# One decoder layer with cross attention and experts on one core: GpSimd's routing and norm application go to ScalarE, DMA and VectorE, and every fourth head's probabilities are turned by TensorE

## The chip, the cores and the metric

The kernel runs on one core of a Trainium2 chip. The metric is the device time of one execution in microseconds. Three runs of the kernel before took 1084.84, 1085.49 and 1087.52 us; the median is 1085.49.

## The reference

The input `x` is 32 x 64 x 256 and the context `ctx_2048` has the same shape, so there are 2048 tokens of width 256. Three sublayers follow each other, each on the layer norm of its input and each added to it.

```python
x = x + attn(_layernorm(x))              # 16 heads attend to one another inside each token, with rope
x = x + xattn(_layernorm(x), ctx_2048)   # 2048 queries against 2048 keys, 16 heads of 16
x = x + moe(_layernorm(x))               # a shared expert, and the best 2 of 8 routed ones
```

In the cross attention queries, keys, probabilities and values are quantised: q and k per row to 127 steps, the probabilities unsigned to 255 steps of the row's largest, v to 127 steps. In the expert layer each token has a sigmoid score per expert; the two experts whose score plus bias is largest are chosen, and the token times its score goes through the expert's `silu(x w1) * (x w3)` and `w2` in bf16.

## The kernel before, in words

128 tokens are a tile, so there are 16 tiles. A prologue prepares keys and values of the whole context in SBUF. Then `over_tiles` runs a body 18 times. The body is written once for each engine, by hand, and each engine executes its list strictly in order and waits on semaphores. In body `t` four tiles are worked on at once: the cross attention of tile `t`; the preparation of `a = t + 2` (first norm, q, k, v, rope, the scores inside a token) and of `n = t + 1` (values inside a token, output projection, second norm, queries); the end of the attention, the third norm and the routing of `m = t - 1`; the experts of `o = t - 2`. The 16 heads `h` of tile `t` are the clock of the body: everything else hangs on a head number.

For one head TensorE makes 128 x 2048 scores in two halves (`scores`, L1528). Each half is a slot of 1024 words in PSUM, and there are two slots, used in turn (`score_uses`, `wait_slot`). VectorE evicts each half with its minimum (`keep_scores`, L1178) and makes a bias (`bias`, L1188). ScalarE takes the exponential (`exp_head`, L865) into `prob`, a ring of four. SP issues a DMA that turns the 128 x 2048 fp16 rectangle into `prob_t`, a ring of six (`turn`, L431). TensorE multiplies four heads at a time by the values (`times_values`, L1558).

GpSimd's list for a tile, in order: `ln_scale(0, a)`, `value_products(2, n)`, `spread_sums(m)`, which waits for VectorE's `cross_sum` (`sum_inv`, L1195) at head 3, `value_products(3, n)` and folds, `rope(a)`, `norm_ho(n)`, `score_products(0, a)`, `ln_scale(2, m)`, more products and folds, `ln_scale(1, n)`, `choose(m)`, folds, `route(0, m)`, `shift_scores(a)`, `route(1, m)`, `value_products(0, a)` and `(1, a)`, folds. `shift_scores(a)` waits for VectorE's `largest_score(a)` (`hs_max`, L1119), which stands just ahead of head 15's eviction. `ln_scale(kind, t)` makes the inverse deviation from VectorE's statistics (`var_eps` L462, `rstd` L466) and applies the norm (`normed`, L482). TensorE turns `normed` (`ln_turn`, L1391) and ScalarE copies it out (`ln_keep`, L809).

`choose` ranks the eight scores of a token in 12 instructions on GpSimd (L523 to L556). TensorE spreads the gates over the partitions at heads 13 and 14 (`spread_gates`, L1605), ScalarE copies them to SBUF (`keep_gates`, L916), and GpSimd multiplies the turned tokens by them (`route`, L567) into `routed_t`. `experts(i, j)` multiply four experts each (L1386): (0, 0) at head 14 of body `m + 1`, the others at heads 0 and 1 of the next body. ScalarE takes their tanh (`hidden_tanh`, L923): group 0 at head 14, group 1 at the start of head 0. VectorE forms the product (`expert_hidden`, L1235 and L1238): group 0 at head 0, group 1 at head 1. Then follow `experts_out` and `add_out` at head 2. The last tile has its own forms on VectorE (`choose_last`, `route_last`).

Of the kernel before, what the change touches and what calls it, by code (L numbers as in the profile page):

```python
# [36 lines left out]
F32 = mybir.dt.float32  # L37
# [26 lines left out]
POOL_NORMS = (0, 1, 2)  # L64
BY_DMA = tuple(range(H))
# [70 lines left out]
def layer_kernel(nc, a):  # L136
    with ExitStack() as ctx:
# [14 lines left out]
        earlier = sb("earlier", [P, E, E])  # L152
# [87 lines left out]
        gate = sb("gate", [P, 3, E])  # L240
        ahead = sb("ahead", [P, E, E])
        beats = sb("beats", [P, E, E])
        ties = sb("ties", [P, E, E])
        routed_gate = sb("routed_gate", [P, E])
        last_gate = sb("last_gate", [P, 4, E])

        routed_both = sb("routed_both", [P, 2, E * D], BF16)
        gate_wide = routed_both[:, 0, :].bitcast(F32).rearrange("p (e q) -> p e q", e=E)
# [110 lines left out]
        last_chain = sem("last_chain")  # L359
        gate_spread = sem("gate_spread")  # L360
        gate_kept = sem("gate_kept")
        routed_kept = sem("routed_kept")
# [19 lines left out]
        def _(sp):  # L382
# [15 lines left out]
            for buf, name in ((w_o, "w_o"), (w_xq, "w_xq"), (b_xq, "b_xq"), (w_p, "w_p"),  # L398
                              (b_p, "b_p"), (w_gate, "w_gate"), (b_expert, "b_expert"),
                              (earlier, "earlier"), (w_s1, "w_s1"), (w_s3, "w_s3"),  # L400
                              (w_s2, "w_s2")):
                sp.dma_start(buf[:], a[name]).then_inc(w_loaded, 16)
# [29 lines left out]

            def body(t):
                for h in range(H):
                    if t.exists() and by_dma(h):
                        turn(h, t)
                    if h == 9 and (t + 3).exists():
                        load_x(t + 3)
                    if h == 4 and (t + -2).exists():
                        store(t + -2)  # L440
# [8 lines left out]
        def _(pool):  # L449
# [5 lines left out]
            def ln_scale(kind, t):  # L455
# [3 lines left out]
                if kind not in POOL_NORMS and (due := t.due(1)) is not None:  # L459
                    pool.wait_ge(ln_done[kind], due)  # L460
                    pool.sem_inc(settled, 1)
# [8 lines left out]
                if kind not in POOL_NORMS:  # L470
                    pool.tensor_scalar(shift[:, kind:kind + 1], mean_var[:, kind, 0:1],
                                       rstd[:, kind:kind + 1], -1.0, ALU.mult, ALU.mult
                        ).then_inc(ln_shifted[kind], 1)
                    return
                if kind > 0:
                    pool.wait_ge((one_done, two_done)[kind - 1], t.count(1, 1))
                    pool.sem_inc(settled, 1)
                if (due := t.due(1)) is not None:
                    pool.wait_ge(ln_turned[kind], due)
                    pool.sem_inc(settled, 1)  # L480
# [30 lines left out]

            def choose(t):


                pool.wait_ge(gate_tanhed, t.count(1, 1))
                pool.sem_inc(settled, 1)
                if (due := t.due(2)) is not None:
                    pool.wait_ge(gate_spread, due)
                    pool.sem_inc(settled, 1)
                sig, biased, rank = gate[:, 0, :], gate[:, 1, :], gate[:, 2, :]  # L520
                mine = biased.unsqueeze(2).to_broadcast([P, E, E])
                others = biased.unsqueeze(1).to_broadcast([P, E, E])
                pool.tensor_scalar(sig, gate_tanh[:], 0.5, 0.5, ALU.mult, ALU.add).then_inc(gate_chain, 1)  # L523
                pool.wait_ge(gate_chain, t.count(12, 1))
                pool.sem_inc(settled, 1)
                pool.tensor_tensor(biased, sig, b_expert[:], ALU.add).then_inc(gate_chain, 1)
                pool.wait_ge(gate_chain, t.count(12, 2))
                pool.sem_inc(settled, 1)
                pool.tensor_tensor(ahead[:], others, mine, ALU.subtract).then_inc(gate_chain, 1)
                pool.wait_ge(gate_chain, t.count(12, 3))  # L530
                pool.sem_inc(settled, 1)
                pool.tensor_scalar(ties[:], ahead[:], 0.0, None, ALU.is_equal).then_inc(gate_chain, 1)
                pool.tensor_scalar(beats[:], ahead[:], 0.0, None, ALU.is_gt).then_inc(gate_chain, 1)
                pool.wait_ge(gate_chain, t.count(12, 5))
                pool.sem_inc(settled, 1)
                pool.tensor_tensor(ties[:], ties[:], earlier[:], ALU.mult).then_inc(gate_chain, 1)
                pool.wait_ge(gate_chain, t.count(12, 6))
                pool.sem_inc(settled, 1)
                pool.tensor_tensor(beats[:], beats[:], ties[:], ALU.add).then_inc(gate_chain, 1)
                pool.wait_ge(gate_chain, t.count(12, 7))  # L540
                pool.sem_inc(settled, 1)
                pool.tensor_tensor(ties[:, :, 0:4], beats[:, :, 0:4], beats[:, :, 4:8], ALU.add
                    ).then_inc(gate_chain, 1)
                pool.wait_ge(gate_chain, t.count(12, 8))
                pool.sem_inc(settled, 1)
                pool.tensor_tensor(ties[:, :, 4:6], ties[:, :, 0:2], ties[:, :, 2:4], ALU.add
                    ).then_inc(gate_chain, 1)
                pool.wait_ge(gate_chain, t.count(12, 9))
                pool.sem_inc(settled, 1)
                pool.tensor_tensor(rank, ties[:, :, 4], ties[:, :, 5], ALU.add).then_inc(gate_chain, 1)  # L550
                pool.wait_ge(gate_chain, t.count(12, 10))
                pool.sem_inc(settled, 1)
                pool.tensor_scalar(rank, rank, 2.0, None, ALU.is_lt).then_inc(gate_chain, 1)
                pool.wait_ge(gate_chain, t.count(12, 11))
                pool.sem_inc(settled, 1)
                pool.tensor_tensor(routed_gate[:], rank, sig, ALU.mult).then_inc(gate_chain, 1)  # L556

            def route(i, t):

                pool.wait_ge(gate_kept, t.count(2, i + 1))  # L560
                pool.sem_inc(settled, 1)
                pool.wait_ge(ln_kept[2], t.count(1, 1))
                pool.sem_inc(settled, 1)
                if (due := t.due(4)) is not None:
                    pool.wait_ge(hidden_made, due)
                    pool.sem_inc(settled, 1)
                pool.tensor_tensor(routed_t[:, EG * i:EG * i + EG],  # L567
# [1238 lines left out]
```

## Time and profile before

| | |
|---|---|
| median of three runs | 1085.49 us |
| profiled execution | 1091.66 us |
| its span | 1089.9 us |
| mean granted TensorE clock | 0.865 |
| VectorE, GpSimd busy | 906.8, 854.3 us |
| TensorE matmul, ScalarE busy | 754.3, 686.6 us |
| DMA queue of SP, share of 16 engines | 72.4% |

The profiled execution is one run; its span is shorter than its time by what lies around it, 1.8 us. Busy shares are means over the whole run. PE is TensorE, DVE VectorE, ACT ScalarE, POOL GpSimd, SP the engine that issues the DMAs. A row of a timeline is start, duration, engine, line, operation, output and inputs, count, and in brackets how long the engine had been idle and what ended it.

### The profile page before, as it was taken

The page shows a single profiled execution, that of the slowest core. Times are in us where ns is not written, and L with a number is a line of the kernel's source. Part 1 is how long each engine was busy: PE and PEld are TensorE (multiplying, and loading weights), DVE is VectorE, ACT ScalarE, POOL GpSimd, SP SyncE. Part 2 cuts the span into 40 slices and gives each one's busy share as a digit, 9 for nine tenths or more (in the row PEclk, how much of TensorE's full clock was granted, in tenths as well). Part 3 has the DMA queues.
Part 4 walks back from the last instruction along what each step waited for, and adds up shares of the span by engine and source line. Part 5 has one row for each costly group of instructions (what it writes and reads, how often), then busy time and mean ns, then how long its engine had stood idle before and what let it go on. Part 6 is the DMA issues. An engine that isn't in the chain of part 4 may idle for free.

```text
span 1089.9 us, 21862 instructions
## 1 busy us (share of the span) xinstructions
PE 754.3 (69%) x7250; PEld 438.0 (40%) x7328; DVE 906.8 (83%) x1802; ACT 686.6 (63%) x843; POOL 854.3 (78%) x874
## 2 busy tenths in 40 slices
PE   7956667676667577676656777676768677677565
PEld 4533314344334344344333444344334344334244
DVE  4996889797979889796979889696978889798983
ACT  2534667675757667575768667575666667567761
POOL 7658989797988979797989979797988979763030
PEclk9975779897979989797989879797988979788988
DMA  6012879686986969596877869596876969588991
GB/s 221 1 39 66 163 130 171 125 166 116 167 146 121 168 117 167 111 168 118 163 143 138 159 117 172 106 168 117 162 146 118 178 115 168 97 160 150 165 175 24
DMA packets 540888, 147.71 MB, mean 136 GB/s; under 512 B 534116, under 2 KB 538727, under 8 KB 540391
## 3 DMA queue, kind: packets, MB, share of 16 engines
q1 hardware_dynamic: 540774, 146.31, 72.4%
q8 instruction: 58, 0.95, 0.4%
q14 instruction: 56, 0.45, 0.1%
HBM read 9.96 MB, written 2.10 MB: 11 GB/s over the span
## 4 chain that ended last, share of the span: by engine, by line
issue 31%; POOL 29%; PE 19%; DVE 16%; ACT 2%; POOLq 1%; DMA 1%; SPq 0%; DVEq 0%; ACTq 0%
POOL product L594 14%; DVE score L1178 8%; PE ps L1605 4%; PE ps L1386 4%; POOL normed L482 3%; PE ps_score L1528 3%; POOL folded L612 3%; POOL rstd L466 2%; POOL qk_sin L581 2%; PE ps_score L1386 2%; POOL qk_rot L583 2%; PE ps L1502 1%; PE ps L1507 1%; DVE q_parts L1161 1%; PE ps L1391 1%
## 5 line engine op out<-in xcount | busy, mean ns | idle before, releaser
L1178 DVE TENSOR_SCALAR_CACHE_REDUCE score<-ps_score,q_neg 128x1024 f32<-128x1024 f32 x512 | 636.4, 1276 | 92.6 <-PE ps_score L1528 92.6
L865 ACT ACTIVATE prob<-score,exp_bias 128x2048 uint16<-128x2048 f32 x256 | 512.1, 2001 | 100.8 <-DVE exp_bias L1188 94.5
L1528 PE MATMUL ps_score<-keys,queries 128*128 128x512 bf16 x946 | 319.9, 424 | 178.7 <-DVE score L1178 165.2
L1528 PEld LDWEIGHTS ps_score<-keys,queries 128*128 128x128 bf16 x1024 | 77.7, 103 | 308.9 <-DVE score L1178 239.3
L604 POOL TENSOR_TENSOR folded<-product 128x512 f32<-128x512 f32 x128 | 158.7, 1263 | 2.7 <-DVE hs L1114 1.7
L594 POOL TENSOR_TENSOR product<-hs_exp,v_tok 128x1024 f32<-128x1024 f32 x64 | 149.7, 2353 | 1.6 <-ACT hs_exp L830 1.6
L594 POOL TENSOR_TENSOR product<-qk_rot 128x1024 f32<-128x1024 f32 x64 | 149.0, 2342 | 0.2 <-POOL qk_rot L587 0.2
L567 POOL TENSOR_TENSOR routed_both<-normed_t,routed_both 128x1024 bf16<-128x1024 f32 x30 | 70.6, 2356 | 33.7 <-ACT routed_both L916 33.2
L612 POOL TENSOR_TENSOR folded<-folded 128x256 f32<-128x256 f32 x128 | 92.6, 746 | 0.0
L1391 PE MATMUL ps<-ident,normed 128*128 128x128 f32 x96 | 24.8, 347 | 89.1 <-POOL normed L482 82.5
L809 ACT COPY normed_t<-ps 128x256 f32<-128x256 f32 x48 | 17.6, 366 | 100.8 <-PE ps L1391 100.8
L1558 PEld LDWEIGHTS ps_pv<-prob_t,values 128*32 128x32 f16 x4096 | 60.1, 99 | 31.6 <-issue 31.6
L1558 PE MATMUL ps_pv<-prob_t,values 128*32 128x128 f16 x4096 | 71.4, 224 | 1.9 <-DMA prob_t<-prob 1.9
L1188 DVE TENSOR_SCALAR exp_bias<-low 128x1 f32<-128x1 f32 x256 | 53.9, 210 | 5.3 <-issue 0.3
L1391 PEld LDWEIGHTS ps<-ident,normed 128*128 128x128 f32 x96 | 12.0, 164 | 109.6 <-POOL normed L482 100.8
L916 ACT COPY routed_both<-ps 128x512 f32<-128x512 f32 x30 | 17.4, 584 | 60.0 <-PE ps L1605 59.7
L1386 PE MATMUL ps<-routed_both,w 128*128 128x128 bf16 x512 | 41.4, 227 | 18.2 <-POOL routed_both L567 13.9
L1605 PE MATMUL ps<-ident,routed_gate 128*128 128x128 f32 x256 | 54.0, 398 | 0.0
L1605 PEld LDWEIGHTS ps<-ident,routed_gate 128*128 128x128 f32 x256 | 52.1, 310 | 0.1
L1386 PEld LDWEIGHTS ps<-routed_both,w 128*128 128x128 bf16 x512 | 33.2, 102 | 41.5 <-POOL routed_both L567 28.8
L865 ACT ACTIVATION_READ_ACCUMULATOR prob<-score,exp_bias 128x1 f32 x256 | 48.2, 188 | 0.0
L462 POOL TENSOR_SCALAR var_eps<-mean_var 128x1 f32<-128x1 f32 x48 | 12.8, 267 | 38.8 <-DVE mean_var L1106 37.8
(138 smaller groups left out, 1216.2 us busy)
## 6 DMA issues: line engine op xcount, KB each, us to landing
prob_t<-prob SPq DMA_TRANSPOSE x256, 4.5
prob_t<-in_w SPq DMA_DIRECT2D x3, 1024.0 KB, 4.8
x_in<-in_x SPq DMA_DIRECT2D x16, 128.0 KB, 3.0
score<-in_cond_t SPq DMA_DIRECT2D x4, 512.0 KB, 6.9
out<-x_out SPq DMA_DIRECT2D x16, 128.0 KB, 2.5
w_qkv<-in_w_qkv SPq DMA_DIRECT2D x1, 768.0 KB, 4.2
early<-in_w_kv SPq DMA_DIRECT2D x1, 512.0 KB
w_s<-in_w_s SPq DMA_DIRECT2D x3, 128.0 KB
```

The costliest lines, as they stand in the source:

```text
L567: pool.tensor_tensor(routed_t[:, EG * i:EG * i + EG], normed_t[:, 2].unsqueeze(1).to_broadcast([P, EG, C, P]), gate_wide[:, EG * i:EG * i ...
L594: pool.tensor_tensor(product[:, i % 2], a_, b_, ALU.mult).then_inc(multiplied, 1)
L604: pool.tensor_tensor(folded[:, r], product[:, r, :, :, 0:HD // 2], product[:, r, :, :, HD // 2:HD], ALU.add).then_inc(fold_done, 1)
L612: pool.tensor_tensor(folded[:, r, :, :, 0:HD // 4], folded[:, r, :, :, 0:HD // 4], folded[:, r, :, :, HD // 4:HD // 2], ALU.add).then_inc( ...
L865: act.activation(prob[:, s, :].bitcast(U16), score[:, s, :], ACT.Exp, bias=exp_bias[:, s:s + 1], scale=-1.0, accum_out=prob_sum[:, t.par, ...
L1178: dve.tensor_scalar(score[:, s, HALF * i:HALF * i + HALF], ps_score[:, score_slot(t.count(H, h), i)].rearrange("p b k -> p (b k)"), q_neg[ ...
L1188: dve.tensor_scalar(exp_bias[:, s:s + 1], low[:, s, 0:1], low[:, s, 1:2], LN255, ALU.min, ALU.add).then_inc(bias_ready, 1)
L1386: mm = pe.matmul(out, lhs[c], rhs[c], start=start and c == 0, stop=stop and c == C - 1)
L1391: mm = pe.transpose(out[:, P * c:P * c + P], src[:, P * c:P * c + P], ident[:])
L1528: mm = pe.matmul(ps_score[:, score_slot(n, i), b, :], queries[:, t.par, h // 2, h % 2, :], keys[:, h // 2, k0:k0 + KEYS], start=True, stop ...
L1558: mm = pe.matmul(out[j], beside_zeros(values, i, h + j), prob_t[:, t.count(H, h + j) % KEPT, i, :], start=(i == 0 and first), stop=(i == T ...
L1605: mm = pe.matmul(bank[6 + i][:, P * e:P * e + P], routed_gate[:, EG * i + e:EG * i + e + 1] .to_broadcast([P, P]), ident[:], start=True, s ...
```

## The change

`BY_DMA` leaves out heads 3, 7, 11 and 15. These are turned by 16 TensorE transposes into a score slot and copied to `prob_t` by ScalarE, both two heads later (heads 5, 9, 13, and 1 of the next body). The code for it, `turn` and `keep_turned`, was there already, as were `ln_apply` and the `shift` in `ln_scale`.

GpSimd's `normed` is gone for all three norms: `ln_scale` ends with a 128x1 `shift`, and ScalarE's `ln_apply` writes `normed`: norm 0 at head 1, norm 2 at head 8, norm 1 at head 10.

GpSimd's `choose` and `route` are gone. VectorE's six instructions of `choose_last` become `choose` for every tile, at head 10. ScalarE multiplies `normed` by each expert's gate, eight `route` instructions at heads 12 and 13. SP issues one DMA that turns the resulting 128 x 2048 bf16 rectangle. The spread gates, their copies and `route_last` are gone.

The order moves: `experts(0, 0)` from head 14 to head 0 of the next body, `experts(1, 1)` from head 1 to 2, `experts_out` and `add_out` from 2 to 3, `hidden_tanh` from heads 14 and 0 to the start of heads 1 and 2, `expert_hidden` from heads 0 and 1 to 1 and 2, `queries_or_keys(0)` from head 3 to 4.

```diff
-POOL_NORMS = (0, 1, 2)
-BY_DMA = tuple(range(H))
+BY_DMA = tuple(h for h in range(H) if h % 4 != 3)
...
+            def turn_routed(t):
+
+                sp.wait_ge(routed_made, t.count(E, E))
+                sp.sem_inc(settled, 1)
+                if (due := t.due(4)) is not None:
+                    sp.wait_ge(hidden_made, due)
+                    sp.sem_inc(settled, 1)
+                sp.dma_start_transpose(routed_t.rearrange("p e c q -> p (e c) q"),
+                                       routed_tok.rearrange("p e d -> p (e d)")).then_inc(routed_turned, 16)
...
+                    if (t + -1).exists() and h == 13:
+                        turn_routed(t + -1)
                     if t.exists() and by_dma(h):
                         turn(h, t)
...
-                x = (x_in[:, t.par, :], x_one[:, t.par, :], x_two[:])[kind]
-                pool.tensor_scalar(normed[:, kind, :], x, mean_var[:, kind, 0:1], rstd[:, kind:kind + 1],
-                                   ALU.subtract, ALU.mult).then_inc(ln_done[kind], 1)
+                pool.tensor_scalar(shift[:, kind:kind + 1], mean_var[:, kind, 0:1],
+                                   rstd[:, kind:kind + 1], -1.0, ALU.mult, ALU.mult
+                    ).then_inc(ln_shifted[kind], 1)
...
+            def route(e, t):
+
+                if e == 0:
+                    act.wait_ge(gate_chain, t.count(6, 6))
+                    if (due := t.due(16)) is not None:
+                        act.wait_ge(routed_turned, due)
+                act.activation(routed_tok[:, e, :], normed[:, 2, :], ACT.Copy, scale=routed_gate[:, e:e + 1]
+                               ).then_inc(routed_made, 1)
...
-                    if o.exists() and h == 0:
-                        hidden_tanh(1, o)
+                    if o.exists() and h in (1, 2):
+                        hidden_tanh(h - 1, o)
...
+                    if m.exists() and h in (12, 13):
+                        for e in range(EG * (h - 12), EG * (h - 12) + EG):
+                            route(e, m)
...
+                    if m.exists() and h == 8:
+                        ln_apply(2, m)
+                    if n.exists() and h == 10 + late:
+                        ln_apply(1, n)
...
-                    if o.exists() and h == 0:
+                    if o.exists() and h == 1:
                         expert_hidden(0, o)
...
+                    if m.exists() and h == 10:
+                        choose(m)
...
                     if o.exists() and h == 0:
+                        experts(0, 0, o)
                         experts(0, 1, o)
```

On ScalarE `keep_turned` stands near the start of a head, before the routes; at head 13 `keep_queries` is ahead of both. At head 10 `ln_apply(1)` is ahead of `gate_tanhs`. All of them are ahead of the head's own exponential.

## Rows read from the trace of the kernel before

**Rows 1.** The page: busy time, share of the span and instructions.
```profile
PE 754.3 (69%) x7250; PEld 438.0 (40%) x7328; DVE 906.8 (83%) x1802; ACT 686.6 (63%) x843; POOL 854.3 (78%) x874
```
**Rows 2.** The page: the chain that ended last, shares by engine.
```profile
issue 31%; POOL 29%; PE 19%; DVE 16%; ACT 2%; POOLq 1%; DMA 1%; SPq 0%; DVEq 0%; ACTq 0%
```
**Rows 3.** Timeline of GpSimd, one tile.
```profile
561.60 0.22 POOL L462 TENSOR_SCALAR var_eps<-mean_var 128x1 f32<-128x1 f32 x1
...
563.27 1.24 POOL L482 TENSOR_SCALAR normed<-x_one,mean_var,rstd 128x256 f32<-128x256 f32 x1 [0.69 <-POOL rstd L466]
564.59 0.20 POOL L523 TENSOR_SCALAR gate<-gate_tanh 128x8 f32<-128x8 f32 x1
...
569.61 2.47 POOL L604 TENSOR_TENSOR folded<-product 128x512 f32<-128x512 f32 x2
...
573.74 2.35 POOL L567 TENSOR_TENSOR routed_both<-normed_t,routed_both 128x1024 bf16<-128x1024 f32 x1 [0.30 <-issue]
```
**Rows 4.** Stretches: length, PE, PEld, DVE, ACT, POOL busy, clock, DMA, GB/s.
```profile
556.16:577.58 21.42, 11.54 (x142) 6.97 (x136) 14.96 (x31) 11.29 (x12) 16.82 (x24) 0.84 0.59 114
577.58:591.44 13.86, 8.66 (x160) 4.95 (x148) 13.72 (x28) 10.23 (x14) 13.01 (x11) 1.00 0.87 154
517.93:577.58 59.65, 38.17 (x411) 22.08 (x412) 52.55 (x108) 40.27 (x49) 53.37 (x55) 0.94 0.78 146
```
**Rows 5.** Timeline of VectorE: bias of head 10, first eviction of head 0.
```profile
556.16 0.21 DVE L1188 TENSOR_SCALAR exp_bias<-low 128x1 f32<-128x1 f32 x1
...
581.62 1.28 DVE L1178 TENSOR_SCALAR_CACHE_REDUCE score<-ps_score,q_neg 128x1024 f32<-128x1024 f32 x1
```
**Rows 6.** Timeline of TensorE: a slot refilled, a turn of `normed`, eight transposes.
```profile
544.44 0.60 PE L1528 MATMUL ps_score<-keys,queries 128*128 128x512 bf16 x2 [0.60 <-DVE score L1178]
...
564.56 0.69 PE L1391 MATMUL ps<-ident,normed 128*128 128x128 f32 x2 [4.93 <-POOL normed L482]
...
571.18 0.62 PE L1507 MATMUL ps<-ident_bf,q_parts 128*128 128x128 bf16 x8 [1.51 <-DVE q_parts L1161]
```
**Rows 7.** Timeline of VectorE: `sum_inv` of bodies 1, 7 and 14.
```profile
165.34 0.24 DVE L1195 RECIPROCAL sum_inv<-prob_sum 128x16 f32<-128x16 f32 x1
...
531.85 0.24 DVE L1195 RECIPROCAL sum_inv<-prob_sum 128x16 f32<-128x16 f32 x1
...
961.37 0.24 DVE L1195 RECIPROCAL sum_inv<-prob_sum 128x16 f32<-128x16 f32 x1
```
**Rows 8.** Groups of ScalarE's instructions: busy us, mean ns, idle before.
```profile
L847 ACT COPY queries<-ps 64x1024 bf16<-64x1024 bf16 x32 | 32.2, 1006 | 1.9 <-PE ps L1507 1.5
L923 ACT ACTIVATE early<-ps 128x512 f32<-128x512 f32 x32 | 18.6, 581 | 5.9 <-PE ps L1386 4.3 <-DVE early L1238 1.5
L809 ACT COPY normed_t<-ps 128x256 f32<-128x256 f32 x48 | 17.6, 366 | 100.8 <-PE ps L1391 100.8
```
**Rows 9.** The tile `prob_t`: from a DMA's issue to its landing.
```profile
DMA to landing us min/median/max: 4.2/4.5/7.5
```
**Rows 10.** Stretches, as in rows 4, while TensorE was idle.
```profile
562.00:564.00 2.00, 0.00 (x0) 0.00 (x0) 0.03 (x2) 0.00 (x0) 1.30 (x2) 0.50 0.47 90
```
**Rows 11.** Timeline of ScalarE: the exponential of head 0.
```profile
584.59 2.00 ACT L865 ACTIVATE prob<-score,exp_bias 128x2048 uint16<-128x2048 f32 x1 [1.23 <-DVE exp_bias L1188]
```
**Rows 12.** Timeline of GpSimd in body 1: `spread_sums` and norm 1.
```profile
165.76 0.52 POOL L509 COPY sum_wide<-sum_inv 128x128 f32<-128x128 f32 x2 [0.25 <-DVE sum_inv L1195]
...
169.36 2.49 POOL L604 TENSOR_TENSOR folded<-product 128x512 f32<-128x512 f32 x2 [0.76 <-DVE ho L1137]
...
193.62 0.22 POOL L462 TENSOR_SCALAR var_eps<-mean_var 128x1 f32<-128x1 f32 x1
```
**Rows 13.** Timeline of VectorE: `choose_last`, its first and last instruction.
```profile
1076.88 0.17 DVE L1210 TENSOR_SCALAR last_gate<-gate_tanh 128x8 f32<-128x8 f32 x1 [5.30 <-ACT gate_tanh L904]
...
1077.89 0.17 DVE L1222 SCALAR_TENSOR_TENSOR routed_gate<-last_gate 128x8 f32<-128x8 f32 x1
```
**Rows 14.** TensorE's waits by line: us in total, times, longest.
```profile
PE ps_pv L1558 <- DMA prob_t<-prob: 1.9, 1, 1.9
```

More of the change, by code:

```diff
@@ L239, in layer_kernel @@
         gate_tanh = sb("gate_tanh", [P, E])
[L240 to L243, printed above, removed]
+        gate = sb("gate", [P, 4, E])
         routed_gate = sb("routed_gate", [P, E])
[L245 removed]
         routed_both = sb("routed_both", [P, 2, E * D], BF16)
[L248 removed]
+        routed_tok = routed_both[:, 0, :].rearrange("p (e d) -> p e d", e=E)
         routed_t = routed_both[:, 1, :].rearrange("p (e c q) -> p e c q", e=E, c=C)
@@ L458, in ln_scale @@
                 pool.sem_inc(settled, 1)
-                if kind not in POOL_NORMS and (due := t.due(1)) is not None:
+                if (due := t.due(1)) is not None:
                     pool.wait_ge(ln_done[kind], due)
@@ L510, in spread_sums @@
                                      of.unsqueeze(3).to_broadcast([P, G, 2, HD])).then_inc(sum_spread, 1)
[L512 to L567, printed above, removed]
-                                   normed_t[:, 2].unsqueeze(1).to_broadcast([P, EG, C, P]),
-                                   gate_wide[:, EG * i:EG * i + EG, :].unsqueeze(2).to_broadcast([P, EG, C, P]),
-                                   ALU.mult).then_inc(routed_kept, 1)
@@ L668, in body @@
                     ln_scale(1, n)
-                if m.exists() and t.exists():
-                    choose(m)
                 if a.exists():
@@ L960, in body @@
                         ln_keep(1, n)
+                    if a.exists() and h == 1 + behind:
+                        ln_apply(0, a)
                     if a.exists() and h == 2 + behind:
@@ L975, in _ @@
             first, second = Tile(0), Tile(1)
-            if 0 not in POOL_NORMS:
-                ln_apply(0, first)
+            ln_apply(0, first)
             ln_keep(0, first)
@@ L984, in _ @@
                     head_exp(first)
-                if u == 5 and 0 not in POOL_NORMS:
+                if u == 5:
                     ln_apply(0, second)
@@ L994, in _ @@
                 if u == 9:
-                    if 1 not in POOL_NORMS:
-                        ln_apply(1, first)
+                    ln_apply(1, first)
                     ln_keep(1, first)
@@ L1204, in cross_norm, with choose @@
                                   xo_raw[:].rearrange("p c q -> p (c q)"), ALU.mult).then_inc(xo_done, 1)
-            def choose_last(t):
-                sig, biased, marked, best = (last_gate[:, i, :] for i in range(4))
+            def choose(t):
+                sig, biased, marked, best = (gate[:, i, :] for i in range(4))
                 dve.wait_ge(gate_tanhed, t.count(1, 1))
-                dve.tensor_scalar(sig, gate_tanh[:], 0.5, 0.5, ALU.mult, ALU.add).then_inc(last_chain, 1)
-                dve.wait_ge(last_chain, 1)
+                dve.tensor_scalar(sig, gate_tanh[:], 0.5, 0.5, ALU.mult, ALU.add).then_inc(gate_chain, 1)
+                dve.wait_ge(gate_chain, t.count(6, 1))
@@ L1706, in body @@
                         gate_and_shared(1, m)
-                    if m.exists() and h == 14:
-                        experts(0, 0, m)
                     if a.exists() and h == 6:
```

118 lines of the change are left out of this document (30 added, 88 removed).

## The prediction

> **What bounds the kernel now.** I read the busy line first, then the chain of waits, then one tile of each engine in order of time. VectorE is busiest (83%) with GpSimd behind it (78%) [rows 1], which names no bound. The chain names one: the largest engine share is GpSimd's 29%, and most of its "issue" lies between GpSimd instructions; VectorE has 16% [rows 2]. The tile from 518 to 578 us shows it: GpSimd runs nearly without a gap, `var_eps` of the second norm, `normed`, twelve small instructions of `choose` (564.59 to 569.61), folds, `route(0)` of 2.35, `hs`, `route(1)` [rows 3]. In that tile VectorE is busy 52.55 of 59.65 us, and of the 7.1 that are left 6.5 lie after 556.16 [rows 4], most of them at head 12, where a score matmul stands behind the turn of `normed` on TensorE, which waited 4.93 us for GpSimd [rows 6]. So a tile is GpSimd's list. From the sum_inv of body 1 to that of body 14 there are 13 tiles in 961.37 - 165.34 = 796.0 us, 61.2 each [rows 7].
>
> I count a tile from S, the first eviction of head 15 (577.58 in the trace, where the first stretch of [rows 4] ends and the second begins), to the next S. `hs_max` just ahead of S releases GpSimd's next list.
>
> **What leaves GpSimd.** `choose` 5.0 us, two routes 4.7, three `normed` (1.24 each, 0.27 for the `shift` that replaces it, priced as `var_eps`) 2.9 [rows 3]: 12.6 us a tile. If that list were still the bound, a tile would lose over 10 us. But GpSimd is then held by others: `spread_sums` waits for `sum_inv` at head 3, `hs` for `hs_max` at head 15. A tile becomes a loop through four engines, which I walk.
>
> **A. S to the first eviction of head 0.** Before: 4.04 us (577.58 to 581.62), with `expert_hidden(0)` in it [rows 5]. Now `experts(0,0)` and `(0,1)` stand on TensorE ahead of head 0's scores and wait for the routed transpose, which SP issues after the eighth `route` on ScalarE. Those are at head 13 behind `keep_queries` (two copies of 1.0 us) and `keep_turned(11)` (the same 1024 words a partition, so 1.0) [rows 8]. The queries reach ScalarE 0.8 us after T13 (head 13's first eviction), so: 0.8 + 2.0 + 0.9 + 4 routes of 0.3 (a 128x256 copy takes 0.37 [rows 8] and the next starts 0.1 earlier) = T13 + 5.0. T13 to S is 2.66 + 0.5 + 3.13 + 0.4 = 6.7. So the routes end at S - 1.7. Transposes of this size land 4.2 to 7.5 us after issue, median 4.5 [rows 9]: I take 4.5, so S + 3.0. No row has a transpose of `routed_tok`; its rectangle is that of `prob`. Then two expert groups 0.9 and a score pair 0.6: head 0 is evicted from S + 4.6, at half clock S + 5.9. TensorE has been idle over 3 us by then, and in its idle stretch before 564.56 the granted clock fell to 0.50, which is 1.2 GHz [rows 6, 10]. I take 5.2. If the landing were hidden, the step would be 2.7.
>
> **B. Head 0 to head 1.** Before 3.1 us. Now VectorE takes `expert_hidden(0)` before head 1's eviction, and its tanh stands on ScalarE at head 1, behind `exp(0)`, which starts only after `bias(0)`: 2.97 us after head 0's first eviction (581.62 to 584.59), 2.0 long [rows 5, 11]. Tanh 0.6 more [rows 8], then the product pair 1.35 and `ln_combine` 0.13: 7.05 in all. 2.7 of it is pure waiting, and every piece has a row.
>
> **C. Head 1 to `sum_inv`.** Before 6.7 us (13.86 from S to `sum_inv` [rows 4], less 4.04 and 3.1). Now head 15 is turned here. Its sixteen transposes take one of the two score slots. TensorE can start when head 1's first half is evicted, +1.34 (eviction 1.28 and a semaphore); eight such transposes took 0.62 [rows 6], so sixteen 0.9 to 1.1, and 1.8 at half clock. Normally a slot is refilled 0.6 us after its eviction with 0.4 us to spare [rows 6]; with the turn between them head 2 starts 0.5 late at full clock and 1.6 at half. ScalarE: `keep_turned` 0.9, `ln_apply(0)` 0.3, `exp(1)` 2.0, `keep_xo` 0.3, then `hidden_tanh(1)` 0.6; only then `expert_hidden(1)` 1.3. That makes 7.95 us at full clock, 9.65 at half; I take 9.2, since TensorE has by then waited some 5 us. S to `sum_inv` becomes 5.2 + 7.05 + 9.2 = 21.45, where it was 13.86.
>
> **D. GpSimd from `sum_inv` to the last `shift`.** In the one tile where `spread_sums` waited for `sum_inv` it began 0.42 after it (165.34 to 165.76), and `var_eps` of norm 1 came at 193.62: 27.86, less a fold wait of 0.76, of which I keep 0.1, less 1.0 for `normed` of norm 2: 26.2 [rows 7, 12]. `var_eps` to the end of `shift` is 1.65. ScalarE's `ln_apply(1)` and `gate_tanh` 0.5. `gate_tanhs` stands behind `ln_apply(1)` in ScalarE's list at head 10, so VectorE, which now does `choose` at head 10, waits for this chain. VectorE's own work from `sum_inv` to `choose` is 556.16 - 531.85 = 24.3 us [rows 5, 7], plus turns at heads 5 and 9 (0.5 to 0.6 each) and smaller delays, 25.7, against 28.8 on this path: it waits some 3 us and GpSimd sets the step.
>
> **E. `choose` to the next S.** `choose` as six VectorE instructions took 1.2 us (1076.88 to 1077.89 and its end) [rows 13]. From `bias(10)` to S was 21.42 us, of which VectorE was busy 14.96 [rows 4, 5], 15.2 with its short gaps. Plus the turn at head 13, 0.7: 17.1.
>
> **Sum.** 21.45 + 0.4 + 26.2 + 1.65 + 0.5 + 17.1 = 67.3 us a tile, 6.1 over 61.2: 13 tiles, +79 us.
>
> **Where I cost nothing.** The spread-gate matmuls and their two copies go, but they lay between heads 12 and 14, where the loop now waits for VectorE. Twelve transposes in place of sixteen unload the DMA queue, yet TensorE waited 1.9 us on it in the whole run [rows 14], so at most 1.9 comes back. `ln_apply(0)` and `(2)` on ScalarE: 0.4 each, inside steps C and D; without cover they would be 0.8 a tile. Both query projections at head 4 end before head 5's slot is free. SP's queue: the routed transpose is issued before head 13's, which is not ready by then; the `x_out` store moves one head and nobody waits for it.
>
> A rule bears on the turned heads. The Trainium skill (VectorE: DVE Perf Modes, "The three transpose paths") gives a 128x128 transpose 390 ns on TensorE and 1309 ns by DMA, and its rule for authors prefers TensorE where PSUM may take the result. By these figures sixteen blocks would be an estimated 6.2 us against 21; the trace has all sixteen by DMA landing in 4.5 us and eight on TensorE in 0.62, so it agrees on the order and on neither size. By the rule the time would fall; by the trace the DMA is hidden and the slot is not.
>
> **The ends.** Up to body 1's `sum_inv`: +0.5. Body 14, which has no list of GpSimd's to wait for: steps A to C +7.6, turns 1.8, `choose` and its wait 1.8, less about 2.8 for a hole behind TensorE like that of [rows 6], which goes: +8.4. Body 15: turns 1.6, `choose` 1.2, less part of such waits: +2. The last two bodies: head 15 through TensorE saves some 2 us against the DMA's landing; eight routes and a transpose (2.4 + 4.7) stand where the spread and `route_last` took 3.5 us: +3. Together +14. So 1091.7 + 93 = 1184.7 for an execution like the profiled one. That one lies 6.2 above the median of the runs: 1178.5, which I give as 1178.
>
> **The mechanism's own range.** At full clock in A and C a tile is 65.4 and the ends +10: 1149. At half clock in A, C, at head 13 and in the query projection it is about 69.8 and the ends +17: 1214.
>
> **Rivals.**
> Only part of the waits is real (the routed transpose is hidden, B stays): a tile of 63 to 64.5, total 1120 to 1145. For it: DMA lands as early as 4.2. Against: ScalarE's order at head 13. 0.13.
> Half clock throughout A, C and E: 1205 to 1215. For it: the clock fell after 4.93 us of idleness, and the loop has three such holes. Against: one hole is only 3.3 us. 0.12.
> The loop holds but the expert steps are hidden: 67.3 less A's 2.5, B's 2.7 and C's 2.0 is about 60, total near 1082. The lists' order speaks against it. 0.05.
> The other side: VectorE alone becomes the bound. Its work a tile (52.55 busy and short gaps, 53.0) plus `choose` 1.2 and turns 2.1 gives 56.3; 13 tiles save 64 us, ends +8: 1091.7 - 56 - 6 = 1030. It decides as soon as A, B and the gate wait together cost under 5 us a tile, that is if `sum_inv` comes before S + 17. For it: 12.6 us leave the engine that the chain names. Against: `exp(0)` cannot start before `bias(0)`. 0.10. The Trainium skill (Perfetto Trace Analysis, "Optimizing GPSIMD Operations") advises to prefer other engines over GpSimd; this rival is what that advice would give here, and the trace agrees on the engine's load.
>
> **Chances.** Forecast 0.60, and the rivals as given. No change means within 0.3%. Slower 0.85, same 0.05, faster 0.10. The range 1130 to 1208 leaves out the two cases below and the highest end of the clock case.
>
> **What would show it.** Right: VectorE waits about 2.7 us for the tanh `early` ahead of head 1 and 1 us or more at head 2; about 3 us for `gate_tanh` at head 10; TensorE waits 2 to 4 us for the routed transpose; GpSimd waits over 8 us a tile for `hs_max`; `sum_inv` 67 us apart. Wrong: `sum_inv` 60 us apart or less, or no wait of VectorE for ScalarE at head 1.

## The result and the profile after

The changed kernel takes 1215.99 us (median of 4 runs, 1214.42 to 1219.45), the kernel before 1086.03 beside it: a ratio of 1.12, 95% interval 1.1172 to 1.1228. The direction was forecast, the size was not: 38 us are missing, and the range ended at 1208.

The page after: busy times, the DMA queue, the chain by engine (it answers [rows 1, 2]).

```profile
PE 818.5 (67%) x8096; PEld 478.0 (39%) x8096; DVE 923.4 (76%) x1905; ACT 804.5 (66%) x1053; POOL 692.7 (57%) x664
...
q1 hardware_dynamic: 440790, 121.11, 53.6%
...
issue 23%; DVE 20%; PE 19%; POOL 18%; ACT 11%; DMA 7%; SPq 1%; POOLq 0%; DVEq 0%; ACTq 0%
```

GpSimd lost 162 us of work, and no engine fills more than 76% of the span: the chain now runs through all of them. These are pieces of it in order of time (start, us, what), from the shift of norm 1 to the steps after the next S (625.29):

```profile
606.78 0.28 POOL shift L474
607.28 0.31 issue
607.59 0.17 ACT gate_tanh L828
607.78 0.18 DVE gate L1137
...
617.80 1.29 DVE score L1105 x2
619.23 1.88 PE ps_score L1453 x16
621.30 0.74 issue
622.04 1.71 ACT routed_both L842 x4
623.90 4.35 DMA routed_both<-routed_both
628.30 1.89 PE ps L1301 x16
...
636.17 0.49 ACT early L849
636.68 0.70 DVE early L1155
...
639.51 1.88 PE ps_score L1453 x16
641.41 1.02 ACT prob_t L801
...
646.27 0.61 ACT early L849
646.91 0.70 DVE early L1155
```

The reader sees every step of the forecast in one chain: GpSimd's shift releases the gate's tanh (D), `choose` and the evictions up to the turn of head 11 (E), four routes, the DMA and the first experts (A), the tanh (B), the turn of head 15, its copy and the second tanh (C). VectorE's waits in that stretch, from its timeline (the number in brackets is the wait and what ended it):

```profile
607.78 0.17 DVE L1137 TENSOR_SCALAR gate<-gate_tanh 128x8 f32<-128x8 f32 x1 [3.19 <-ACT gate_tanh L828]
...
621.83 1.28 DVE L1105 TENSOR_SCALAR_CACHE_REDUCE score<-ps_score,q_neg 128x1024 f32<-128x1024 f32 x1 [1.28 <-PE ps_score L1443]
...
631.09 1.28 DVE L1105 TENSOR_SCALAR_CACHE_REDUCE score<-ps_score,q_neg 128x1024 f32<-128x1024 f32 x1 [3.06 <-PE ps_score L1443]
...
636.68 0.69 DVE L1155 SCALAR_TENSOR_TENSOR early<-early,ps 128x512 f32<-128x512 f32 x1 [2.64 <-ACT early L849]
...
642.26 1.28 DVE L1105 TENSOR_SCALAR_CACHE_REDUCE score<-ps_score,q_neg 128x1024 f32<-128x1024 f32 x1 [1.45 <-PE ps_score L1443]
...
646.91 0.69 DVE L1155 SCALAR_TENSOR_TENSOR early<-early,ps 128x512 f32<-128x512 f32 x1 [2.07 <-ACT early L849]
...
648.36 0.24 DVE L1122 RECIPROCAL sum_inv<-prob_sum 128x16 f32<-128x16 f32 x1
```

The waits by line (us in all, times, longest) say the same of the whole run. At these two places GpSimd now waits 20 us a tile together:

```profile
POOL hs L481 <- DVE hs_max L1046: 172.8, 16, 12.7
POOL sum_wide L502 <- DVE sum_inv L1122: 157.4, 16, 44.7
DVE gate L1137 <- ACT gate_tanh L828: 43.4, 16, 4.8
```

The same two places in the kernel before, under 4 us a tile together:

```profile
POOL hs L488 <- DVE hs_max L1119: 41.1, 16, 3.8
POOL sum_wide L509 <- DVE sum_inv L1195: 18.1, 3, 13.3
```

With `sum_inv` of body 1 at 165.85 and of body 14 at 1062.74 (VectorE's timeline) 13 tiles take 896.9 us, 69.0 each, where [rows 7] give 61.2. I take the steps apart by the starts of the evictions, as the prediction did, and average over 13 tiles, from the S ahead of body 2 to that ahead of body 15; so S to S comes out 0.1 under the 69.0 from `sum_inv` to `sum_inv`:

| step, us a tile | predicted | measured |
|---|---|---|
| A: S to head 0 | 5.2 | 5.54 |
| B: head 0 to head 1 | 7.05 | 6.99 |
| C: head 1 to `sum_inv` | 9.2 | 9.52 |
| D: `sum_inv` to `choose` | 28.75 | 28.93 |
| E: `choose` to S | 17.1 | 17.91 |
| S to S | 67.3 | 68.9 |

### The profile page after: what moved, and what is told of

It is laid out like the page before. It is cut to its first block, busy times and chain, and to the rows that moved or that the text cites. A ratio compares the mean times of both kernels' runs of the same rounds, so it can differ in the third digit from the quotient of the medians.

```text
span 1214.1 us, 23321 instructions
## 1 busy us (share of the span) xinstructions
PE 818.5 (67%) x8096; PEld 478.0 (39%) x8096; DVE 923.4 (76%) x1905; ACT 804.5 (66%) x1053; POOL 692.7 (57%) x664
## 4 chain that ended last, share of the span: by engine, by line
issue 23%; DVE 20%; PE 19%; POOL 18%; ACT 11%; DMA 7%; SPq 1%; POOLq 0%; DVEq 0%; ACTq 0%
DVE score L1105 12%; POOL product L527 10%; DMA routed_both<-routed_both 6%; PE ps_score L1453 5%; PE ps L1301 5%; ACT routed_both L842 3%; PE ps_score L1443 3%; ACT prob L789 3%; POOL qk_sin L514 2%; POOL folded L545 2%; DVE early L1155 2%; PE ps_score L1301 2%; POOL qk_rot L516 1%; ACT early L849 1%; POOL rstd L470 1%
## 5 line engine op out<-in xcount | busy, mean ns | idle before, releaser
L1443 PE MATMUL ps_score<-keys,queries 128*128 128x512 bf16 x1024 | 361.9, 447 | 149.2 <-DVE score L1105 129.4
L1453 PE MATMUL ps_score<-ident_f,prob 128*128 128x128 f16 x1024 | 93.6, 264 | 98.9 <-DVE score L1105 98.9
L1453 PEld LDWEIGHTS ps_score<-ident_f,prob 128*128 128x128 f16 x1024 | 81.3, 120 | 126.2 <-issue 126.0
L801 ACT COPY prob_t<-ps_score 128x1024 int32<-128x1024 int32 x64 | 64.8, 1012 | 86.6 <-PE ps_score L1453 85.7
L481 POOL TENSOR_TENSOR hs<-hs,hs_max 128x256 f32<-128x256 f32 x16 | 9.9, 621 | 172.8 <-DVE hs_max L1046 172.8
L502 POOL COPY sum_wide<-sum_inv 128x128 f32<-128x128 f32 x32 | 8.4, 292 | 157.4 <-DVE sum_inv L1122 157.4
L1301 PE MATMUL ps<-routed_both,w 128*128 128x128 bf16 x512 | 49.8, 265 | 57.1 <-DMA routed_both<-routed_both 55.4
L1155 DVE SCALAR_TENSOR_TENSOR early<-early,ps 128x512 f32<-128x512 f32 x32 | 22.0, 688 | 72.0 <-ACT early L849 62.1
L1301 PEld LDWEIGHTS ps<-routed_both,w 128*128 128x128 bf16 x512 | 43.7, 123 | 78.7 <-DMA routed_both<-routed_both 63.0
L842 ACT ACTIVATE routed_both<-normed,routed_gate 128x256 bf16<-128x256 f32 x128 | 54.2, 496 | 0.0
```

Of the source, the lines that this page charges most:

```text
L801: act.copy(prob_t[:, t.count(H, h) % KEPT].rearrange("p k q -> p (k q)").bitcast(I32), ps_score[:, turn_slot(t.count(H, h))].rearrange("p ...
L842: act.activation(routed_tok[:, e, :], normed[:, 2, :], ACT.Copy, scale=routed_gate[:, e:e + 1]).then_inc(routed_made, 1)
L1301: mm = pe.matmul(out, lhs[c], rhs[c], start=start and c == 0, stop=stop and c == C - 1)
L1443: mm = pe.matmul(ps_score[:, score_slot(n, i), b, :], queries[:, t.par, h // 2, h % 2, :], keys[:, h // 2, k0:k0 + KEYS], start=True, stop ...
L1453: mm = pe.transpose(out[:, P * i:P * i + P], prob[:, h % RING, P * i:P * i + P], ident_f16[:])
```

## The experiments

The time is the median of 4 to 10 runs. In brackets stand its ratio to the kernel before, on the same chip, and the 95% interval of the ratio. Steps and tiles are read from the profiled run.

**e1, turns undone.**
```diff
-BY_DMA = tuple(h for h in range(H) if h % 4 != 3)
+BY_DMA = tuple(range(H))
```


> The changed kernel, but all sixteen heads are turned by DMA again, so no turn takes a score slot and ScalarE copies none. Loop theory (a tile is S to sum_inv, GpSimd's list to the shift of norm 1, the gate, choose to S): step C loses its turn and copy (10.3 to about 8), step E the turn at head 13 (17.5 to about 16.2), step A starts 1.0 earlier because the copy ahead of the routes is gone. About 4.4 us a tile less than 69.0, with the ends 1155, between 1140 and 1175. Rival 'the turns are the loss': the time falls to 1095 or below. Rival 'given back': with 17 DMA turns a tile the landing gets later and the time stays above 1205.

1180.42 (1.0849, 1.0812 to 1.0887). 36 us came back, not 61. By steps: C 8.58, E 16.23, but D holds at 28.84, since GpSimd's list is what it was, and VectorE's waits for the gate grew from 43.4 us in all to 58.6. A rose to 5.91. What VectorE gains between `sum_inv` and the gate is given back at the gate.

**e2, the expert products one head later on VectorE.**
```diff
-                    if o.exists() and h == 1:
+                    if o.exists() and h == 2:
                         expert_hidden(0, o)
...
+                    if o.exists() and h == 3:
+                        expert_hidden(1, o)
                     if t.exists():
                         keep_scores(h, t)
```


> The changed kernel, but VectorE takes expert_hidden(0) at head 2 and expert_hidden(1) at head 3, one head later, so that ScalarE's tanh is long done. Loop theory: the two waits for the tanh (2.65 and 2.07 us in the tile looked at) lie between S and sum_inv, which releases GpSimd's list, so they count in full: 4.4 us a tile, 14 times, 62 us less: 1154, between 1140 and 1175. Rival 'not on the path' (GpSimd's list is released by hs_max, or the wait for the gate takes it up): 1216 within 4, and the wait for gate_tanh grows by what the tanh waits lose.

1143.68 (1.0515, 1.0481 to 1.0548): 72 us from moving two pairs of instructions. B is 3.07 and C 6.77, as before the change. D rose to 30.78: the second pair now stands on VectorE between `sum_inv` and `ho`, a reduction that GpSimd's next fold needs, so GpSimd waits for `ho` 1.8 us a tile (1.0 us in the whole run of the changed kernel):
```profile
POOL folded L537 <- DVE ho L1064: 25.5, 14, 2.3
```

**e3, the gate's tanh ahead of `ln_apply(1)`.**
```diff
-                    if n.exists() and h == 10 + late:
-                        ln_apply(1, n)
                     if m.exists() and h == 10:
                         gate_tanhs(m)
+                    if n.exists() and h == 10 + late:
+                        ln_apply(1, n)
```


> The changed kernel, but at head 10 ScalarE takes the gate's tanh ahead of ln_apply(1), so choose no longer stands behind GpSimd's norm 1. Loop theory: VectorE's wait of about 3.2 us for gate_tanh goes, 13 tiles, 42 us less: 1174, between 1165 and 1190, and the wait for gate_tanh falls under 0.5 us a tile. Rival 'it only moves': ScalarE waits for the shift just behind it, ahead of the exponential of head 10, and TensorE at head 12 waits for the turned norm, so the time stays at 1216 within 5.

1186.05 (1.0899, 1.0859 to 1.094): 30 of the 42. D fell from 28.93 to 26.18, and the wait is 0.00 in the 13 tiles.

**e4, the kernel before with the norms alone** (`POOL_NORMS = ()`, `ln_apply` at heads 1, 8, 10).

> The kernel before with one part of the change: ScalarE applies the three norms (heads 1, 8 and 10), routing and turns as before. By step D of the prediction GpSimd's list loses 2.9 us a tile and GpSimd set the tile: 13 times, up to 38 us less, of which some comes back where ScalarE waits for the shift at head 10: 1055, between 1045 and 1070. Rival 'ScalarE pays': ln_apply waits for GpSimd ahead of an exponential and the time rises to 1090 to 1110. Rival 'covered': 1086 within 3.

1060.04 (0.976, 0.9705 to 0.9815): this part makes the kernel faster, by 2 to 3%; a tile is 58.6.

**e5, the kernel before with the turns alone** (`BY_DMA` as in the change).

> The kernel before with one part of the change: heads 3, 7, 11 and 15 are turned by TensorE and copied by ScalarE. GpSimd sets the tile there and hardly waits for VectorE, so a turn's slot delay is hidden as long as VectorE has its 7 us of slack: 1092, between 1085 and 1100. Rival 'a turn costs the same everywhere' (the run with all heads by DMA gave 36 us for them in the changed kernel): 1120 or more. Rival 'relief of the DMA queue': below 1083.

1104.41 (1.015, 1.0105 to 1.0195), between the forecast of 1085 to 1100 and the rival's 1120.

**e6, routing alone** (e1 with `normed` on GpSimd again).

> The changed kernel with its norms applied by GpSimd as before and all heads turned by DMA: only routing and the order of the expert steps are changed. Loop theory: A (about 5), B (7) and C (8) stay, but nothing of norm 1 stands ahead of the gate's tanh, so VectorE's own work sets the rest: 20 + 25.7 + 16.2 = 62 us a tile and ends +8: 1105, between 1090 and 1125. Rival 'the parts add up' (1216 less 36 for the turns, plus 27 for the norms): 1207.

1154.1 (1.061, 1.0565 to 1.0656): neither the 1105 nor the 1207. A, B and C stayed (5.16, 7.13, 8.69), D fell to 24.6, but E was 19.14: the first two instructions of `choose` took 1.18 and 1.62 us on average for 0.17 (why stands under e15). The parts sum to -27 + 16 + 66 = +55 us where the whole is +130: 75 us come only when they stand together. Norms and routing together (e1) cost 93 instead of 39. Norm 1 ahead of the gate's tanh is one reason, worth 30 us in the changed kernel (e3); the rest of the 75 was not taken apart.

**e7, all three waits taken away:** e2 and e3, and
```diff
-                    if o.exists() and h == 0:
-                        experts(0, 0, o)
-                        experts(0, 1, o)
...
-                    if o.exists() and h == 0:
+                    if o.exists() and h == 1:
+                        experts(0, 0, o)
+                        experts(0, 1, o)
                         experts(1, 0, o)
```


> The changed kernel with all three waits of the loop taken away: expert_hidden one head later, the gate's tanh ahead of ln_apply(1), and experts(0,0), (0,1) and (1,0) moved from ahead of head 0's scores to behind head 1's. Turns, norms and routing stay where the change put them. Loop theory: 72 and 30 as measured for the first two, 3 us a tile for the third, 40: 1074 if all add up, and not under 1045, where VectorE's work with turns (56.3 us a tile) is reached; 1080, between 1060 and 1100. Rival 'the engines and slots are the loss' (turns, routes and clock on their own): 1120 or more.

1096.75 (1.0081, 1.0052 to 1.011). 119 of the 130 us go though every operation stays on the engine that the change gave it. The loss is order, not load. Its tile is 60.4, from a profiled run of 1103.44 that is the slowest of eight, and still below the 61.2 of before; what is left is in the ends (`sum_inv` of body 14 to the end 145.8 us, 128.5 before).

**e8, TensorE kept busy** with ten products into bank 5 ahead of the wait in `experts(0, 0)`.
```diff
+                    for _ in range(10):
+                        pe.matmul(bank[5][:, :], queries[:, t.par, 0, 0, :], keys[:, 0, 0:KEYS], start=True, stop=True)
```


> The changed kernel, but TensorE makes ten extra 128x512 bf16 products into the bank that experts(0,0) will overwrite, while it waits for the routed transpose (about 2.2 us of its 3 us of idleness a tile); their results are not used. If the lower clock after the idle stretch is a cost, the experts (1.89 us for 16 products), the scores behind them and the turn of head 15 (1.86) speed up: 1.5 to 2 us a tile, 1216 becomes 1190, between 1180 and 1205. Rival 'the clock costs nothing here': 1216 within 5.

1208.72 (1.1093, 1.1031 to 1.1155): 7 us, where 26 were forecast. TensorE's timeline with the filling:

```profile
623.07 2.32 PE L1518 MATMUL ps<-keys,queries 128*128 128x512 bf16 x10
626.74 1.07 PE L1301 MATMUL ps<-routed_both,w 128*128 128x128 bf16 x16 [1.35 <-DMA routed_both<-routed_both]
627.65 1.03 PE L1443 MATMUL ps_score<-keys,queries 128*128 128x512 bf16 x4
...
636.70 1.86 PE L1453 MATMUL ps_score<-ident_f,prob 128*128 128x128 f16 x16 [5.26 <-DVE score L1105]
```

The experts take 1.07 instead of 1.89 (the granted clock there is 1.00 and not 0.50), but the turn of head 15 behind a hole of 5.26 us is still 1.86 at 0.50, and so are most turns of head 11: one of three slow places was mended.

**e9, e7 without e3.**

> The changed kernel with expert_hidden one head later (1144 by itself) and experts(0,0), (0,1) and (1,0) behind head 1's scores in place of ahead of head 0's; the gate's tanh stays behind ln_apply(1). Loop theory: the wait for the routed transpose ahead of head 0's scores (3 us a tile) goes, 14 times, with a little back from the slots: 1110, between 1095 and 1125. Rival 'already covered': 1135 or more, since the scores of head 1 or the tanh are late in its place.

1130.33 (1.0394, 1.0366 to 1.0423): 13 us better than e2, not 34. A fell from 5.96 to 2.75, but D rose from 30.78 to 32.38 and C by 0.5. GpSimd waits for `sum_inv` only 4 times in this run, none of them in the middle tiles. It waits for `ho` instead, 3.0 us a tile; in one tile that I looked at, VectorE waits 1.42 us for the second tanh ahead of `ho`:
```profile
POOL folded L537 <- DVE ho L1064: 42.2, 14, 3.6
```
So part of the wait moved from A into D. No run has e2 and e3 together without this step, so what it is worth with the gate freed (e7) is not shown.

**e10, e7 with all heads by DMA.**

> The changed kernel with all three waits taken away (1097) and all heads turned by DMA again. VectorE is the bound now, so only what a turn adds to its waits counts: about 1.2 us a tile, 1080, between 1065 and 1095. Rival 'the clock pays it back': without the sixteen-product turns TensorE's granted clock falls (0.80 in the run with all heads by DMA against 0.84) and the time stays at 1097 within 5.

1075.68 (0.9895, 0.9855 to 0.9935): within the range. This is the whole change of norms and routing, in another order and without turns, and it is 1% faster than the kernel before.

**e11, e4 with the gate's tanh first and `choose` on VectorE at head 10;** spread gates and GpSimd's `route` stay.

> The kernel before with the norms applied by ScalarE, the gate's tanh ahead of ln_apply(1), and choose on VectorE at head 10; the spread gates, GpSimd's route, all expert steps and all turns by DMA stay as before. GpSimd's list falls to 61.2 - 2.9 - 5.0 = 53.3 us and VectorE has 54.2 of work, so a tile of about 56.5 and 1035, between 1020 and 1050. Rival 'the gate is late': choose waits on VectorE for the tanh, and the time stays at the 1060 of the norms alone or above.

1059.4 (0.9739, 0.9707 to 0.9771): no gain over e4; the rival's sign is right, its wait is not (0.00 at the gate). GpSimd, 5 us a tile lighter, waits 133.1 us for the spread gates instead.

**e12, e4 with the turns.**

> The kernel before with two parts of the change, norms by ScalarE and every fourth head turned by TensorE; routing as before. If the two add up (-27 and +16): 1077. Rival 'a turn costs what VectorE's slack doesn't cover': with GpSimd's list shorter the slack is gone, and a turn costs the 2 us a tile and more that it cost in the changed kernel: 1095.

1093.39 (1.0049, 1.0031 to 1.0068). The same four turns cost 16 us where GpSimd's list was the bound (e5), 33 here, 36 in the changed kernel (e1) and 21 in e7 against e10: their price is lowest where VectorE, which waits for the slot, had slack. Why it is 21 and not 33 in e7, where VectorE has little, is not shown.

**e13 and e14, one turn undone:** head 11 (`h % 4 != 3 or h == 11`), head 15 likewise.

> The changed kernel, but head 11 is turned by DMA (heads 3, 7 and 15 stay with TensorE). Its turn stands in step E at head 13 and its copy ahead of the routes. By the prediction's price (0.7 in E, and the routes 1.0 earlier in A): 22 us less, 1194. If the turn at half clock is what was mis-sized, E falls by 1.3 to 1.7: 1216 less 14 x 2.3 = 1184. Rival 'free': 1216 within 4.

> The changed kernel, but head 15 is turned by DMA (heads 3, 7 and 11 stay with TensorE). Its turn and copy stand in step C. By the prediction's price (0.5 to 1.6 for the slot, part of 1.0 for the copy): C falls from 9.5 to about 8.2 and the time by 18 to 1198, with some 2 us lost at the very end. Rival 'covered by the tanh': expert_hidden(1) waits for the exponential chain anyway and C falls by less than 0.4: 1212 or more.

1205.31 (1.1093, 1.1057 to 1.1129) and 1205.69 (1.109, 1.1066 to 1.1114), each between its forecast and its rival. Without head 11's turn E is 16.61 for 17.91: that turn costs 1.3, not 0.7, and only half of it reaches the end (A and C rose by 0.2 each). Without head 15's C is 8.63 for 9.52 and A 5.86 for 5.54.

**e15 and e16, no exponential behind GpSimd's shift:** norm 0 on GpSimd, `ln_apply(1)` behind `exp_head` of head 10; e15 with `choose` on VectorE (from e11), e16 without.

> As the run with norms and choose moved (1059), but norm 0 is applied by GpSimd as before and ln_apply(1) stands behind the exponential of head 10 instead of ahead of it, so no exponential waits for GpSimd's shift. If these waits held the tile at 58.9: 56.5 a tile, 1030, between 1015 and 1045. Rival 'spread gates and routes hold it': 1059 within 5.

> The same without the move: choose on GpSimd as in the kernel before, norm 0 on GpSimd, norms 1 and 2 on ScalarE, the gate's tanh ahead of ln_apply(1) and that behind the exponential of head 10. GpSimd's list is 61.2 - 1.94 = 59.3 us a tile: 1062, between 1052 and 1072. If it comes out as e15, the move of choose is worth nothing in any order.

1092.58 (1.0049, 1.0024 to 1.0073) and 1062.94 (0.9777, 0.9757 to 0.9797). e16 is as expected, and no better than e4 (59.0 and 58.6 us a tile). e15 is 33 us slower than e11. E is 22.8 there. VectorE's timeline at `choose`, and GpSimd's beside it:

```profile
552.93 1.84 DVE L1212 TENSOR_SCALAR last_gate<-gate_tanh 128x8 f32<-128x8 f32 x1
554.80 2.24 DVE L1214 SCALAR_TENSOR_TENSOR last_gate<-last_gate,b_expert 128x8 f32<-128x8 f32 x1
557.07 0.17 DVE L1217 MAX8 last_gate<-last_gate 128x8 f32<-128x8 f32 x1
```
```profile
552.39 4.62 POOL L594 TENSOR_TENSOR product<-qk_rot 128x1024 f32<-128x1024 f32 x2
557.10 0.22 POOL L462 TENSOR_SCALAR var_eps<-mean_var 128x1 f32<-128x1 f32 x1
```

Two instructions of 0.17 us last 1.84 and 2.24, and the second ends where GpSimd's two products end (557.01). The Trainium skill (SBUF — State Buffer, "SBUF: two separate sides") says that a GpSimd operation and a VectorE operation in a two-port mode, or with two SBUF inputs while GpSimd reads SBUF, exclude each other: the one that starts first blocks the other for its whole length. The trace agrees for the second instruction, which has two SBUF inputs; the first has one, and no row tells its mode.

**e17 and e18, e15 and e11 with the tanh and the score in PSUM.** TensorE's turn of norm 1 into the same bank then waits for all six steps of `choose`, and not for the tanh alone.
```diff
-        gate_tanh = sb("gate_tanh", [P, E])
+        gate_tanh, gate_sig = bank[5][:, E:2 * E], bank[5][:, 2 * E:3 * E]
```


> As e15 (choose on VectorE, norm 0 on GpSimd, no exponential behind GpSimd's shift), but the gate's tanh and the score lie in PSUM beside the gate's products. If the stall is a lock between VectorE and GpSimd over what both take from SBUF: the two instructions take 0.2 each again, 3.7 us a tile less, 1092.6 becomes 1040, between 1030 and 1055. Rival 'the stall is the operands' late arrival or the instruction itself': they stay at 1.8 and 2.2 and the time stays at 1093 within 5.

> As e11 (norms on ScalarE, choose on VectorE, 1059), with the tanh and the score in PSUM. The first instruction of choose took 1.44 on average there; at 0.2 it gives 1.3 us a tile: 1041, between 1030 and 1052. Rival 'GpSimd and the gates behind choose hold the tile': 1059 within 4.

1063.1 (0.9762, 0.973 to 0.9794) and 1060.11 (0.9751, 0.9708 to 0.9794). In e17 the groups of the two instructions are

```profile
L1212 DVE TENSOR_SCALAR ps<-ps 128x8 f32<-128x8 f32 x16 | 2.7, 171 | 4.8 <-ACT ps L902 4.8
L1214 DVE SCALAR_TENSOR_TENSOR last_gate<-ps,b_expert 128x8 f32<-128x8 f32 x16 | 2.7, 167 | 0.5
```

They take 0.17 though a product of GpSimd's runs beside both in each of the first 13 tiles. So the stall follows where the operands lie, and 29.5 of the expected 52 us come back. With neither the stall nor an exponential behind a shift, e17's tile is still 59.5 and not 56.5: my theory that ScalarE's waits held the tile falls. e18 gains nothing over e11, though 1.3 us of stall a tile went; what took its place was not separated. Nor was what holds these five runs near 1060. In e4 and e16 the list of GpSimd as forecast (58.3 and 59.3) is what the tile takes (58.8 and 59.3 from `sum_inv` to `sum_inv`); in e11, e17 and e18 GpSimd waits for the spread gates instead, 133.1, 129.0 and 142.0 us in all.

## Why the prediction was right in sign and too low

**What failed.** The steps of the loop held, in their places and in their waits; the failed step is the sizing of what TensorE does in it. The forecast took the turn at head 13 at full clock, 0.7 us in E, and a middle of the two clocks in A and C. Measured, that turn is worth 1.3 (e13), and the turns at heads 13 and 1 and the experts run at half clock: E is 17.91 for 17.1, A 5.54 for 5.2, C 9.52 for 9.2. The ends, taken at 13.4 us, came to 22.8, and 6.2 us were taken off that the run after did not give back.

**The bound before** was read rightly: GpSimd's list set the tile. e4 shortens it by 2.9 us and the tile falls by 2.4. But e11 takes 5.0 more off the list and gains nothing: the next bound lay close behind.

**Steps A to E** each exist as forecast: the routes of the tile looked at end 1.55 ahead of S (forecast 1.7), the DMA takes 4.35 us ([rows 9] gave 4.5) and lands 3.0 behind S. There the forecast's own sum had a slip: 4.5 from S - 1.7 is S + 2.8, not the S + 3.0 that it used. VectorE waits 2.64 for the tanh where [rows 11] led to 2.7, and `choose` waits 2.8 to 3.2 in the 13 tiles where 3 were forecast. e2, e3 and e7 show that these waits are most of the loss.

**Where the 38 us are**, worked from the tables above and [rows 7]:
- E, 0.8 a tile: 10.5 us. The turn at head 13 was taken at 0.7 and is worth 1.3 (e13); the slower products around it are argued for the rest. In the tile looked at, the turns at heads 5 and 9 took 1.05 us each, as priced, and those at heads 13 and 1 took 1.86. A stretch of E (length, PE, PEld, DVE, ACT, POOL, clock):
```profile
745.90:764.20 18.30, 13.69 (x112) 6.78 (x112) 15.64 (x39) 14.55 (x20) 3.85 (x4) 0.63 0.40 79
```
  A mean of 0.63 between the levels 0.5 and 1.0 puts most of it at 1.2 GHz; the tile above has an E of 17.51 at 0.81.
- A and C, 0.3 each: 8.6 us. I had taken a middle between full and half clock, but the experts (1.89 for 16 products) and the turn of head 15 (1.86) are at half clock: the granted clock is 0.50 from 628.30 to 630.20 and from 639.50 to 641.40. A route is 0.50 long, and four take 1.70 where I had 1.2:
```profile
L842 ACT ACTIVATE routed_both<-normed,routed_gate 128x256 bf16<-128x256 f32 x128 | 54.2, 496 | 0.0
```
- D, 0.2: 2.3 us. B came out 0.06 under the forecast, -0.8 us.
- The ends: +22.8 from body 14's `sum_inv` on, for 13.4. Body 14 +11.9 (8.4), body 15 +3.3 (2), the last two +7.6 (3). In the last, eight routes take 3.29 us together on ScalarE, and TensorE waits 7.99 until their transpose has landed:
```profile
1197.37 3.29 ACT L842 ACTIVATE routed_both<-normed,routed_gate 128x256 bf16<-128x256 f32 x8
```
```profile
1205.15 2.74 PE L1301 MATMUL ps<-routed_both,w 128*128 128x128 bf16 x24 [7.99 <-DMA routed_both<-routed_both]
```
- 6.2 us I took off because the profiled execution of before lay that far above its median. The one after lies on its median (1216.02).

The steps are 20.6 us from S to S; from `sum_inv` to `sum_inv`, which is how the forecast counted, the 13 tiles are 21.9 over it. 21.9 + 9.4 + 6.2 and 0.5 of rounding are 38.0.

**The rivals.** "Half clock throughout A, C and E" (1205 to 1215, chance 0.12) was nearest, and the range left it out; the forecast's own upper end was 1214, so a range that ended at 1208 was narrower than its own bounds. "VectorE becomes the bound" (1030) is what e7 and e10 approach once the waits are gone: VectorE's share of the chain is 35% and 41% there and 20% in the changed kernel. Even they stay at 60.4 and 59.1 a tile. The forecast saw the hole ahead of the turn at head 1. It did not see the low clock at head 13. In the tile above the granted clock is 0.58 from 610.90 to 613.00, behind 4.81 us in which TensorE is idle, 1.00 from 615.40 to 617.90, and 0.50 at the turn (619.20 to 621.10), though TensorE was idle only for 1.51 and 0.34 us just ahead of it. Why it falls there is not shown.

**Costed at nothing:** that `choose` on VectorE is not slowed by GpSimd held only by the order of the change. There its first two instructions took 0.17 in all 16 tiles, and no GpSimd instruction ran beside them: GpSimd had ended its shift and stood waiting for VectorE's `hs`. Freed from the wait for the gate the first one stalled beside GpSimd's products (0.64 on average in e3, 1.6 in e10; in e15 both, 1.6 and 1.7).

**The rule on transposes** that the prediction quoted from the Trainium skill (VectorE: DVE Perf Modes, "Rules for kernel authors") prefers TensorE. The runs differ: e1, e5, e12 and e10 against e7 all show DMA faster in this kernel, where a turn takes a score slot and a copy of 1.01 us on ScalarE.

## What to carry to other kernels

Before moving work off the engine that the chain names, follow what every engine that takes over its work will wait for: a consumer placed one head too early on the next engine cost more (72 us) than the one part that paid had brought (27). Price a step in a loop by where its wait ends. Where a wait of several microseconds leaves TensorE idle, price the products behind it at the slow clock too, as measured here at heads 0 and 1; at head 13 it was slow behind short holes as well. Test each part alone and then together, for here one part won 27 us, two lost 16 and 66, and together they cost 75 more. Where small VectorE operations run beside a busy GpSimd, try them with PSUM operands: that won 29.5 us in e17 and nothing in e18.

## Not expected of the hardware

VectorE's 128x8 operations of 0.17 us lasted 1.84 and 2.24 us beside GpSimd's 128x1024 products and 0.17 again with an operand in PSUM (e15, e17). Turns on TensorE went with a higher clock: the mean granted clock was 0.801 with all heads by DMA (e1), 0.84 with four turned, 0.876 and 0.844 in e7 and e10; but it was 0.798 with heads 3, 7 and 15 turned (e13) and 0.84 with heads 3, 7 and 11 (e14), so their number alone does not set it. Sixteen transposes took 1.86 us behind a hole (e8's timeline above) and 1.05 at heads 5 and 9.
